# High and low parts of queries and keys written by one instruction each, and later or earlier slots for layer 1's stacks, chunk products, router, expert sums and the future values

## The reference

```python
# layer 0, xn = layernorm(x)
q, k = rope(xn @ Wq.T), rope(xn @ Wk.T)          # 16 heads of 8
probs = softmax(q @ k.T * scale + bias, causal)
out0 = relu(probs + tau / row) @ v @ Wo.T        # tau/row also acts on the masked (future) keys
ffn0 = fp4_linear(silu(fp4_linear(xn, Wg)) * fp4_linear(xn, Wu), Wd)   # blocks of 16 quantized
x = x + out0 + ffn0
# layer 1, xn = layernorm(x)
q, k = elu(rope(q) * SC) + 1, elu(rope(k) * SC) + 1
out1[t] = q[t] @ sum_{s<=t} k[s] v[s]^T / max(q[t] . sum_{s<=t} k[s], 1e-6)
moe = sum over the top 2 of 4 experts, weighted by the router's softmax, plus one shared expert
x = x + out1 @ w_out + moe
```

## Time and profile before

| | us |
|---|---|
| three runs, median (lowest to highest) | 2109.91 (2109.56 to 2110.14) |
| the profiled execution, its device time | 2108.19 |
| its span from the first to the last instruction | 2106.2 |

### The profile page before, as it was taken

How to read it: one execution, slowest core, us unless ns; L and a number is a source line. 1 busy time by engine, 2 the same in 40 slices (tenths; PEclk the granted TensorE clock), 3 DMA queues, 4 the chain that set the end, 5 groups by cost and what they waited for, 6 DMA issues and landing times.

```text
span 2106.2 us, 49813 instructions
## 1 busy us (share of the span) xinstructions
PE 1934.5 (92%) x17353; PEld 1264.0 (60%) x17353; DVE 1540.6 (73%) x5223; ACT 1375.7 (65%) x3861; POOL 1143.8 (54%) x1799
## 2 busy tenths in 40 slices
PE   3789999999999999999999999999999999998978
PEld 1455666656566575666657566575656657565645
DVE  6558778687776868778687877868777686876646
ACT  1677585675857667585766858567685766757531
POOL 4676374655637465473746647475563746545220
PEclk9779999999999999999999999999999999999999
DMA  5102021110301102020210201121030110201010
GB/s 146 27 9 44 4 39 23 34 29 8 54 4 38 24 20 42 4 56 6 39 24 18 44 4 39 23 39 24 10 52 4 38 24 17 40 4 34 4 32 6
DMA packets 172653, 59.37 MB, mean 28 GB/s; under 512 B 139643, under 2 KB 169971, under 8 KB 172403
## 3 DMA queue, kind: packets, MB, share of 16 engines
q1 hardware_dynamic: 172403, 56.19, 13.9%
HBM read 14.22 MB, written 4.19 MB: 9 GB/s over the span
## 4 chain that ended last, share of the span: by engine, by line
PE 56%; ACT 16%; DVE 12%; POOL 8%; issue 7%; DMA 1%; SPq 0%; ACTq 0%; DVEq 0%; POOLq 0%
PE ps L1124 11%; PE ps L1260 8%; PE ps L1195 8%; PE ps L1205 7%; ACT ring L946 5%; PE ps L1138 5%; PE ps L1114 4%; ACT pb L955 3%; PE ps L1245 3%; DVE ring L577 3%; PE ps L1183 2%; DVE lin L609 2%; POOL ring L843 2%; PE ps L1103 2%; PE ps L1171 2%
## 5 line engine op out<-in xcount | busy, mean ns | idle before, releaser
L843 POOL TENSOR_SCALAR ring<-ring,row_rcp,tau_row 128x128 f32<-128x128 f32 (+3 forms) x1024 | 625.5, 618 | 676.1 <-DVE row_rcp L584 676.1
L946 ACT ACTIVATE ring<-ring,neg_max 128x128 f32<-128x128 f32 (+3 forms) x1024 | 570.8, 558 | 504.0 <-DVE neg_max L577 499.4
L1124 PE MATMUL ps<-identf,ring 128*128 128x128 f32 x2560 | 378.6, 287 | 10.4 <-POOL ring L843 7.6
L955 ACT ACTIVATE pb<-ps 128x512 f32<-128x512 f32 x640 | 348.0, 583 | 27.5 <-PE ps L1124 23.2
L1124 PEld LDWEIGHTS ps<-identf,ring 128*128 128x128 f32 x2560 | 279.2, 143 | 83.4 <-issue 39.0
L577 DVE CUSTOM_DVE_ANT_1 ring<-ps,bias_t 128x384 f32<-128x384 f32 (+1 forms) x496 | 286.7, 614 | 53.7 <-PE ps L1114 46.4
L1260 PEld LDWEIGHTS ps<-ed_t,h 128*128 128x128 f32 (+1 forms) x1920 | 254.6, 191 | 97.2 <-issue 93.7
L1260 PE MATMUL ps<-ed_t,h 128*128 128x128 f32 (+1 forms) x1920 | 270.6, 277 | 0.0
L1205 PE MATMUL ps<-xn1T,eu_t 128*128 128x512 f32 (+1 forms) x480 | 256.5, 616 | 1.3 <-DVE h L633 1.2
L1195 PE MATMUL ps<-xn1T,eg_t 128*128 128x512 f32 (+1 forms) x480 | 255.6, 614 | 2.2 <-DVE h L626 2.1
L1114 PE MATMUL ps<-qkT 32*128 32x128 f16 (+3 forms) x1024 | 201.4, 308 | 47.1 <-DVE neg_max L577 28.0
(11 more groups left out here) (152 smaller groups left out, 2815.7 us busy)
## 6 DMA issues: line engine op xcount, KB each, us to landing
x_t<-x SPq DMA_DIRECT2D x16, 256.0 KB, 2.9
x<-x SPq DMA_DIRECT2D x16, 256.0 KB, 2.9
o_rows<-o_stack SPq DMA_DIRECT2D x256, 16.0 KB
out<-x SPq DMA_DIRECT2D x16, 256.0 KB, 2.3
qkT<-qkx SPq DMA_TRANSPOSE x128, 3.2
bias_t<-bias SPq DMA_DIRECT2D x1, 1536.0 KB, 7.8
eg_t<-eg SPq DMA_DIRECT2D x1, 860.0 KB
eu_t<-eu SPq DMA_DIRECT2D x1, 860.0 KB
```

What stands on the lines that cost most here:

```text
L843: pool.tensor_scalar(e, e, row_rcp[:, m % 2, r:r + 1], tau_row[:, i, HG * g + r:HG * g + r + 1], ALU.mult, ALU.add).then_inc(p_ok.sem, 1)
L946: act.activation(e, e, ACT.Exp, bias=neg_max[:, n % 2, r:r + 1], scale=-1.0, accum_out=row_sum[:, n % 2, r:r + 1]).then_inc(exp_ok.sem, 1)
L955: act.activation(pb[:, c % NPB, :], bank(turn_bank(q)), ACT.Relu).then_inc(t_taken[q % 2].sem, 1)
L1124: last = pe.transpose(o[:, r * P:(r + 1) * P], ring_of(i, r)[:, k * P:(k + 1) * P], idf)
```

## The change

The high parts of query and key are written by one ACT instruction instead of two, the low parts by one POOL instruction instead of two, through a helper `parts` that steps over both. The key's low part moves ahead of its two high parts. The semaphores count one step a block instead of two. The quantized input is turned ahead of the query/key/value product of slot 10, into a buffer that it shares with two other users (`qT32`). In layer 1 the high parts are written at slots 27, 28, 30 and 32 instead of 26 to 29, the low parts one slot and the DMA two slots behind them. The chunk products start two slots later and use slot 47, their products with the values lie at 42, 46, 49 and 53. The router lies six slots later, the down products of experts 1 and 2 two and one slots later, the expert sums at 43, 48, 53 and 60. The future values are made at slots 33 and 35 instead of 61 and 63.

```diff
-TURN_H, FUTURE_V, FUTURE_Y = (ATT + 11, ATT + 13, ATT + 13, ATT + 15), ATT + 61, ATT + 63
+TURN_H, FUTURE_V, FUTURE_Y = (ATT + 11, ATT + 13, ATT + 13, ATT + 15), ATT + 33, ATT + 35
-LIN = [L1 + (35, 37, 39, 41, 43, 45, 49, 51)[v // 2] for v in range(H)]
-INTRA = (L1 + 40, L1 + 42, L1 + 46, L1 + 53)
+LIN = [L1 + (37, 39, 41, 43, 45, 47, 49, 51)[v // 2] for v in range(H)]
+INTRA = (L1 + 42, L1 + 46, L1 + 49, L1 + 53)
-ROUTER = L1 + 31
+ROUTER = L1 + 37
-DOWN1 = [GATE1[3 * e + 2] + 4 for e in range(NE - 1)] + [L1 + 65]
+DOWN1 = [L1 + p for p in (35, 44, 49, 56, 65)]
+ADD_EXPERT = [L1 + p for p in (43, 48, 53, 60, 69)]
-TURN_STACK0, TURN_STACK1 = QKV0 + 5, QKV1 + 8
+TURN_STACK0, STACK1 = QKV0 + 5, (L1 + 27, L1 + 28, L1 + 30, L1 + 32)
...
-        xqT = xnT
...
+        xqT = qT32
...
-        hi_ok = two("stack_high", 2 * T)
-        lo_ok = two("stack_low", 2 * T)
+        hi_ok = two("stack_high", T)
+        lo_ok = two("stack_low", T)
...
+        def parts(layer, t, first, step, n):
+
+            v = qkx[layer][:, t, :, :, :]
+            dims = [[step, 2], [R, H]] + ([[HD, n]] if n > 1 else []) + [[1, HD]]
+            return bass.AP(v.tensor, v.offset + first, [list(v.ap[0])] + dims)
...
-                    if 0 <= p - TURN_STACK1 < T:
-                        turn_stack1(b, p - TURN_STACK1)
+                    if p - 2 in STACK1:
+                        turn_stack1(b, STACK1.index(p - 2))
...
-                    if p == DOWN1[e] + 4:
+                    if p == ADD_EXPERT[e]:
                         accumulate(b, e)
...
-                pool.tensor_tensor(qkx[layer][:, t, 0, :, 16:24], q, qkx[layer][:, t, 0, :, 0:8], ALU.subtract).then_inc(lo_ok[layer].sem, 1)
-                pool.tensor_tensor(qkx[layer][:, t, 1, :, 8:16], kk, qkx[layer][:, t, 1, :, 0:8], ALU.subtract).then_inc(lo_ok[layer].sem, 1)
+                both = qk[:, t, :].rearrange("p (a h x) -> p a h x", a=2, x=HD)
+                pool.tensor_tensor(parts(layer, t, 2 * HD, H * R - 2 * HD, 1), both, parts(layer, t, HD, H * R, 1),
+                                   ALU.subtract).then_inc(lo_ok[layer].sem, 1)
...
-                if 0 <= p - QKV1 - 7 < T:
-                    stack_low(b, 1, p - QKV1 - 7)
+                if p - 1 in STACK1:
+                    stack_low(b, 1, STACK1.index(p - 1))
...
-                act.copy(qkx[layer][:, t, 0, :, 0:16].rearrange("p h (a x) -> p h a x", x=HD), q).then_inc(hi_ok[layer].sem, 1)
-                act.copy(qkx[layer][:, t, 1, :, :].rearrange("p h (a x) -> p h a x", x=16)[:, :, :, 0:HD], kk).then_inc(hi_ok[layer].sem, 1)
+                both = qk[:, t, :].rearrange("p (a h x) -> p a h x", a=2, x=HD).unsqueeze(3).broadcast_to([P, 2, H, 2, HD])
+                act.copy(parts(layer, t, 0, H * R + HD, 2), both).then_inc(hi_ok[layer].sem, 1)
...
-                if 0 <= p - QKV1 - 6 < T:
-                    stack_high(b, 1, p - QKV1 - 6)
+                if p in STACK1:
+                    stack_high(b, 1, STACK1.index(p))
...
-                if 0 <= p - QKV0 < T:
-                    qkv(b, 0, p - QKV0)
                 if p == TURN_XQ:
                     pe.wait_ge(x_fp4.sem, x_fp4.at(b, 3))
                     turn(("xq", b, 0), lambda t: xq[:, t * D:(t + 1) * D])
+                if 0 <= p - QKV0 < T:
+                    qkv(b, 0, p - QKV0)
```

More of the change, by code:

```diff
@@ L409, in turn_stack0 @@
             def turn_stack0(b, t):
-                sp.wait_ge(lo_ok[0].sem, lo_ok[0].at(b, 2 * t + 2))
+                sp.wait_ge(lo_ok[0].sem, lo_ok[0].at(b, t + 1))
                 if t == 0 and has(b - 2):
@@ L417, in turn_stack1 @@
             def turn_stack1(b, t):
-                sp.wait_ge(lo_ok[1].sem, lo_ok[1].at(b, 2 * t + 2))
+                sp.wait_ge(lo_ok[1].sem, lo_ok[1].at(b, t + 1))
                 if t == 0 and has(b - 1):
@@ L830, in stack_low @@
             def stack_low(b, layer, t):
-                pool.wait_ge(hi_ok[layer].sem, hi_ok[layer].at(b, 2 * t + 2))
-                q = qk[:, t, 0:D].rearrange("p (h x) -> p h x", x=HD)
-                kk = qk[:, t, D:2 * D].rearrange("p (h x) -> p h x", x=HD)
-                pool.tensor_tensor(qkx[layer][:, t, 0, :, 16:24], q, qkx[layer][:, t, 0, :, 0:8], ALU.subtract).then_inc(lo_ok[layer].sem, 1)
-                pool.tensor_tensor(qkx[layer][:, t, 1, :, 8:16], kk, qkx[layer][:, t, 1, :, 0:8], ALU.subtract).then_inc(lo_ok[layer].sem, 1)
+                pool.wait_ge(hi_ok[layer].sem, hi_ok[layer].at(b, t + 1))
+                both = qk[:, t, :].rearrange("p (a h x) -> p a h x", a=2, x=HD)
+                pool.tensor_tensor(parts(layer, t, 2 * HD, H * R - 2 * HD, 1), both, parts(layer, t, HD, H * R, 1),
+                                   ALU.subtract).then_inc(lo_ok[layer].sem, 1)
             def scale_probs(b, m, r):
@@ L933, in stack_high @@
                         act.wait_ge(st0_ok.sem, st0_ok.at(b, 0))
-                q = qk[:, t, 0:D].rearrange("p (h x) -> p h x", x=HD).unsqueeze(2).broadcast_to([P, H, 2, HD])
-                kk = qk[:, t, D:2 * D].rearrange("p (h x) -> p h x", x=HD).unsqueeze(2).broadcast_to([P, H, 2, HD])
-                act.copy(qkx[layer][:, t, 0, :, 0:16].rearrange("p h (a x) -> p h a x", x=HD), q).then_inc(hi_ok[layer].sem, 1)
-                act.copy(qkx[layer][:, t, 1, :, :].rearrange("p h (a x) -> p h a x", x=16)[:, :, :, 0:HD], kk).then_inc(hi_ok[layer].sem, 1)
+                both = qk[:, t, :].rearrange("p (a h x) -> p a h x", a=2, x=HD).unsqueeze(3).broadcast_to([P, 2, H, 2, HD])
+                act.copy(parts(layer, t, 0, H * R + HD, 2), both).then_inc(hi_ok[layer].sem, 1)
             def exp_with_sum(b, s):
```

## The result

The kernel after takes **2143.42 us** (median, 2141.48 to 2144.18), the one before 2110.02 in the same job: a ratio of 1.0157, 95% interval 1.0145 to 1.0170. It is slower, as forecast, but by 33 us and not 7, outside the range. The profiled span is 2139.5 us (2106.2 before), and a frame takes 126.99 us instead of 124.87, so 15 x 2.12 = 32 of the 33 us stand in the steady frames.

The account below looks back on a forecast made before the run. PE's matmuls, 118.6 of 124.9 us a frame, were taken as the bound. Terms of 0.4 and 0.05 us a frame, times 15, plus 0.5 for the last frame gave about +7 us: 2117 us, range 2113 to 2125.

Parts of the forecast that it names:

- What bounds, and the way a microsecond counts: Whole frame: PE's matmuls bound it, only gaps can be won; a microsecond a frame is worth 15 us in the run.
- Merged parts, quantized input, stacks (0.0): ACT and POOL casts and subtractions, transposes, layer 1's stacks: 0.15 us saved a block each, all hidden, 0.0 a frame.
- The rival in which the casts bound: Slots 25 to 28: lighter ACT shortens the 1.3 us gap before the third state product; 2099 us, faster given 0.3.
- Future values (+0.4): Slots 33 and 35 get 1.0 us longer, slots 61 to 5 return 0.56 us: net +0.4 us a frame.
- the 0.3 us gap at slot 5 then closes: Before the transposes of x: the 0.3 us wait goes, since ACT's part comes some 0.7 us earlier.
- Chunk products, `intra`, experts, router (+0.05): Slots 40 to 52: 0.25 us of new waits less the 0.2 us gap of the second `intra`, +0.05 a frame.
- falls behind PE by 2.1 us: Slots 40 to 43: DVE, with 10.4 us of work against PE's 8.3, becomes the slower and lags 2.1 us.
- it bears a lag of 2.2 us: Slots 44 and 45: PE's 3.4 us of work less 1.2 us for DVE's two maxima absorbs 2.2 us of lag.
- the wait of unit 45's score: Slot 45: the score waits for a chunk product in its bank that DVE must mask; part of 0.25 us of waits.
- The wait of the second expert's first down product for its bank: One slot behind the first expert sum instead of three, this product waits for the bank; part of 0.25 us of waits.
- The rival "DVE binds": Slots 38 to 45: router operations slowed beside POOL make DVE bind; +1.8 us a frame, 2137 us, chance 0.08.
- The last frame (+0.5): The last frame has no scores, so the expert sum is less covered: 0.5 us more, between 0 and 1.7.

Follow-up runs that it names:

- b_merge: The kernel before with only the merged high and low parts and the quantized input turned first, all at the old slots: 2106.74 us, ratio 0.9985.
- b_experts: The kernel before with only the new slots of chunk products, their products with the values, router, down products and expert sums: 2130.41 us, ratio 1.0097.
- a_mul69: The kernel after with POOL's third quantizing product of layer 0's hidden values at slot 69 instead of 68: 2136.20 us, ratio 1.0124.
- a_mul_late: The kernel after with three of POOL's four quantizing products of the hidden values at slots 69, 70, 71 instead of 66, 68, 70: 2135.74 us, ratio 1.0119.
- b_down: The kernel before with only the down products and expert sums moved to their new slots: 2117.54 us, ratio 1.0034.
- a_sum39: The kernel after with the router back at slots 28 and 31 to 37 and the first expert sum at 39 instead of 43: 2136.47 us, ratio 1.0123.
- a_down42: The kernel after with router back at 28 and 31 to 37, first expert sum at 39, second expert's down products at 42: 2138.61 us, ratio 1.0136.
- b_kv33: The kernel before with merged parts and quantized input turned first, plus the third state product at slot 33 instead of 31: 2115.25 us, ratio 1.0026.
- b_gate30: The kernel before with merged parts and quantized input turned first, plus the gate product of slot 31 at 30: 2117.48 us, ratio 1.0037.

## Why the prediction was half right

*What bounds, and the way a microsecond counts.* Right: the change moved no matmul out, and 15 frames carry the loss.

*Merged parts, quantized input, stacks (0.0).* Right: -0.08 a frame. The saving was under-sized: each cast pair saves 0.20 us and each pair of subtractions too, not 0.15. The Trainium skill ("VectorE: DVE Perf Modes", section on the TRN2 errata) gave 0.19 as an estimate from its fixed cost for ScalarE: the two rows, 410 ns for 256 elements and 619 for 512, agree. The rival in which the casts bound did not come: the wait before the third state product did not shrink (17.9 us in the run before, 19.0 in `b_merge`, 19.9 after).

*Future values (+0.4).* It was 0.81. The shape was right: slots 62 and 63 gave back 1.2 us, the scores of units 0 and 1 wait for the row maxima, POOL holds slot 4, and at the transposes behind it 0.33 us were left where 0.26 were forecast. Slots 32 to 37 took 0.97 us more than in `b_experts`, 1.0 forecast. Wrong was the step "the 0.3 us gap at slot 5 then closes". The gap stayed, and slot 5 lost 0.17 us more. The chain's first DVE part did come earlier, 5.45 us behind POOL's first scaling instead of 6.03; but L479 grew from 0.28 to 0.85 us beside POOL's product and ate all of it, so that the row maximum of unit 5 ended 8.04 us behind that scaling in both kernels, and PE's lead was gone at the transposes of x. Where L479 took 0.18 (`a_mul69`, `a_mul_late`) slots 4 and 5 gave back 0.65 us. The prediction read no DVE row between slots 4 and 5.

*Chunk products, `intra`, experts, router (+0.05).* It was 1.39, and here lies most of the miss. The load was right: slots 40 to 43 take 8.64 us instead of 11.08, 2.44 less against 2.5 forecast. Two steps failed. The first is "falls behind PE by 2.1 us": I took the excess of DVE's work over PE's in slots 40 to 43 for a lag, but DVE had idle time there (0.67 us at slot 43 in `b_down`), and the masking of slot 43 started 0.96 us ahead of the next scores with the router and without it. What was lost there was PE's cover, the down quarter of slot 43: the wait of unit 45's score, which the prediction lists, cost 0.38 us. The wait of the second expert's first down product for its bank did not come. The second is "it bears a lag of 2.2 us". I counted the two row maxima against PE's 3.4 us. In the trace, from 1114.80 on, DVE has `silu`, the reciprocals, router, sum and both maxima to do before the chunk products may go on at 1118.72, 3.9 us, against 2.9 us of PE's (1115.26 to 1118.16); and the up product then waits for `h`, DVE's next item, which I had not in the list at all. That is 0.83 us, 1.2 together instead of 0.25. Then come 0.41 us in no row of waits, a term that the sum did not have and whose cause is open, and 0.2 less for the second `intra`, as forecast.

*The rival "DVE binds".* Its result came nearest (2137, +1.8 a frame), its mechanism did not. It needed the router's operations slower beside POOL; together they became shorter (59 to 47 us), the product of two inputs 171 ns instead of 630, with no POOL instruction beside it in any of the sixteen frames. What bound was the row of DVE's instructions in slots 44 and 45, each waiting for the one before. That the two numbers are close is luck.

*The last frame (+0.5).* The span grew by 33.3 us, of which 15 frames make 32: the start and the end hold about 1.5.

## What to carry to other kernels

In a pipeline of fixed slots, an engine that is idle 29% of the span can bind in two slots: before work is moved, write down for each slot pair what every engine has to do in it, all of it, in its order, and not only the instructions that the move touches; a sum of busy time over several slots is not a lag. A wait removed by moving one piece came back elsewhere in four trials here (`a_sum39`, `a_down42`, `b_kv33`, `b_gate30`); what helped was to keep another engine's work off the chain that makes the late value. Where an in-order engine has a long item that nobody waits for, keep it out from in front of one that the bound engine waits for: one sum two slots later was worth 34 us, the falls of the clock among them.

## What the chip showed beyond expectation

A DVE instruction of 32 elements took 182 ns in the mean alone, and 0.85 us beside a POOL product that ended at 1168.38, 0.03 us before it: it looks held until the other's instruction was over. It has only one tensor as input. POOL's recorded start lies 0.04 us behind DVE's, so which came first at the memory the rows don't tell. In the kernel before, the instruction came late beside the same product and ended 0.04 us behind it too (DVE, then POOL), so its 0.28 us there hold 0.1 us of the same wait:

```profile
1148.28 0.28 DVE L472 TENSOR_SCALAR x_step<-x_step 128x32 f32<-128x32 f32 x1
```

```profile
1147.74 0.78 POOL L818 TENSOR_TENSOR hid<-hid,q_step 128x352 f32<-128x352 f32 x1
```

Where only the end of one of POOL's scalings (L849) lay beside it, in `a_mul69`, it took 0.18. The Trainium skill ("SBUF — State Buffer", section "SBUF: two separate sides") states such a lock between VectorE in a two-port mode and GpSimd: whoever comes second waits for the whole instruction. The trace agrees in size, with 182 ns against 768 in the mean of sixteen; that this instruction ran in such a mode no run here shows.

The granted clock fell below 1.00 for the pair of slots 48 and 49 in 7 of 11 frames that had the same work and the same waits, and stayed at 1.00 in the other 4; where it fell, the pair took another 1.6 to 1.7 us (8.82 against 7.16, say), and in one frame 2.9 (10.05 against 7.15). What decides between the frames the rows don't show.
